# Causal mask of layer 1's key-major attention tiles: a GpSimd select on the exponentials in place of mask matmuls

## Chip, cores and metric

One core of one Trainium2 chip. The metric is the device time of one launch in microseconds (us), median of several runs.

## What is computed

Two layers, each `x + s * g`, on `x` of 2 x 1024 tokens and 128 channels. `s` is a 16-head attention with 8 channels a head over the layer-normed tokens, `g` the SiLU of a mixture of experts. The change touches `s` of layer 1 alone:

```
attn = jnp.einsum('bhqd,bhkd->bhqk', Q, K) * scale
causal = jnp.tril(jnp.ones((Sx, Sx), dtype=bool))
attn = jnp.where(causal, attn, jnp.asarray(-jnp.inf, dtype=attn.dtype))
probs = jax.nn.softmax(attn, axis=-1)
y = jnp.einsum('bhqk,bhkd->bhqd', probs, V)
return y @ W_O.T
```

## The kernel before

Every engine runs a program of its own, in the order in which it is written, and semaphores join them. `attention(l)` stands once for each engine. It works through 16 halves H (`HALVES`): a half is 512 queries of one group of four heads (`HG`), so that halves 2G and 2G+1 are the two query ranges of group G.

**Key-major steps.** `t_steps(1, H)` lists a half's steps. An even half has four, one for each tile of 128 keys from 0 to 3, and its rows narrow from 512 queries to 384, 256 and 128, since the queries that come before a key tile are left out. An odd half has eight: tiles 0 to 3 at the full 512 queries, then tiles 4 to 7 at 512, 384, 256 and 128. In the eight steps of a pair that start on the diagonal (all four of an even half, steps 4 to 7 of an odd one) the first 128 columns of each tile need the causal mask. In a step, for each head j:

- TensorE's `st_step` multiplies keys by queries into one of three PSUM banks (4 + m % 3). It waits until the exponential three tiles earlier has left that bank. In layer 1 a diagonal tile gets two more matmuls, `mask(...)`, of 64 rows and 128 columns each, which add -1e30 above the diagonal. Heads 0, 2 and 1, 3 lie in different halves of the array's rows.
- ScalarE (L776) takes the exponential of the tile from PSUM into `Pr`, eight slots of the arena, and counts `e_done`.
- TensorE's `av_step` multiplies V, with a column of ones, by the four exponentials of a step, in four column groups, into bank 7. It is issued one step late: after `st_step(H, i, 2)` TensorE issues `av_step` of the step before.

**Row maxima.** Two halves ahead, the same scores are computed query-major, so that each row's maximum is known: `s_unit` writes one of a ring of four banks (0 to 3), VectorE (L1079) reduces it and frees the bank. These tiles are masked by two matmuls too, with mask and identity changed over. `s_plan` cuts the stream of these units into the steps of each half, `unit_plan[l][H][i]`; TensorE issues them among `st_step` and `av_step`. After a half's last unit stands `("K", H)`, where VectorE joins the two maxima and GpSimd splits them into three bf16 parts (`max_parts`, L662 to L665), and four units later `("M", H)`, where TensorE transposes them (it waits for `mp_ready`); from there they go by DMA into rows of the queries.

**GpSimd in attention.** In each half it first copies V for the next group (`stage`, L648, even halves), then does `max_parts` of two halves ahead, and then `normalise` of the half before (L671), which waits for the inverse sums by DMA (`rb_in`). At the end of a half ScalarE moves bank 7 out (`evac`, L765); the first `av_step` of the next half waits for it.

The diagonal mask's lines in TensorE's program before:

```
masked = l == 1 and kt * P == q0
...
if masked:
    order = (identb, identb_sw) if row == 0 else (identb_sw, identb)
    masks = (mask_kq, mask_kq_sw) if row == 0 else (mask_kq_sw, mask_kq)
    ins = mask(bank(b_, 0, P), row, order, masks)
```

Of the kernel before, what the change touches and what calls it, by code (L numbers as in the profile page):

```python
# [162 lines left out]
def block_net(nc, a, out):  # L163
    ctx = ExitStack()
    with ctx:
# [3 lines left out]
        def sem(name):  # L169
            return ctx.enter_context(nc.semaphore(name))  # L170
# [14 lines left out]
        def bank(n, lo=0, hi=512):  # L185
            return PS[:, n * 512 + lo:n * 512 + hi]
# [85 lines left out]
        def gate_bufs(n):  # L272
# [71 lines left out]
            "ring_full", "ring_free", "st_ps", "e_done", "av_done", "o_ev", "mx_ready", "mp_ready", "v_staged",  # L344
            "sum_in", "sum_inv", "sum_out", "rb_in", "r_done", "pj_ps", "pj_ev")}
            for l in range(2)]
        h_ld = [sem(f"h_ld{s}") for s in range(2)]

        rw_in = [sem(f"rw_in{e}") for e in range(EXP)]
# [22 lines left out]
        def last_s(l, H):  # L372

            return max(place[l][w] for w in s_units(l, H)) + 1

        def two_before(l, H):

# [229 lines left out]
        def _(pool):  # L607
# [31 lines left out]
            def attention(l):  # L639
# [27 lines left out]
                def normalise(H):  # L667
# [2 lines left out]
                    pool.wait_ge(A["rb_in"], 16 * (H + 1))  # L670
                    g.tensor_tensor(OT[:, G, 512 * h:512 * (h + 1)], Osb[:, h, :], RB[l][:, h, :], ALU.mult).then_inc(A["r_done"], 1)  # L671

                stage(0)
                for H in range(LAG[l]):
                    max_parts(H)
                for H in range(HALVES):
                    if H % 2 == 0 and H // 2 + 1 < GROUPS:
                        stage(H // 2 + 1)
                    if H + LAG[l] < HALVES:
                        max_parts(H + LAG[l])  # L680
                    if H >= 1:
                        normalise(H - 1)
                normalise(HALVES - 1)

# [609 lines left out]
        def _(pe):  # L1294
# [57 lines left out]
            def attention(l):  # L1352
# [53 lines left out]
                def st_step(H, i, j):  # L1406
                    kt, off = t_steps(l, H)[i]
                    G, h, pr, row = H // 2, H % 2, j // 2, 64 * (j % 2)
                    m = HG * (steps_before(l, H) + i) + j

                    if m >= 3:
                        pe.wait_ge(A["e_done"], m - 2)
                    w = 512 - off
                    q0 = 512 * h + off
                    b_ = 4 + m % 3
                    extra = []
                    if l == 0 and h == 0 and kt == KT - 2:
                        extra = [(0, Hst[:, G % 2, j, part, 0:P]) for part in range(PARTS)]
                    if l == 0 and h == 0 and kt == KT - 1:
                        extra = [(q * P, Hst[:, G % 2, j, part, P * (1 - q):P * (2 - q)]) for q in range(2) for part in range(PARTS)]  # L1420
                    masked = l == 1 and kt * P == q0
                    ins = mm(bank(b_, 0, w), Ks[G][row:row + TROWS, pr, kt * P:(kt + 1) * P],
                             Qs[G][row:row + TROWS, pr, q0:q0 + w], stop=not (extra or masked))
                    for n, (c0, lhsT) in enumerate(extra):
                        ins = mm(bank(b_, c0, c0 + P), lhsT, flip[:, :], start=False, stop=n == len(extra) - 1)
                    if masked:
                        order = (identb, identb_sw) if row == 0 else (identb_sw, identb)
                        masks = (mask_kq, mask_kq_sw) if row == 0 else (mask_kq_sw, mask_kq)
                        ins = mask(bank(b_, 0, P), row, order, masks)
                    ins.then_inc(A["st_ps"], 1)  # L1430

                def av_step(H, i):
# [2 lines left out]
                    G = H // 2  # L1435
                    n = steps_before(l, H) + i
                    pe.wait_ge(A["e_done"], HG * (n + 1))
                    if i == 0:
                        pe.wait_ge(A["v_staged"], G + 1)
                        if H:  # L1440
                            pe.wait_ge(A["o_ev"], H)
# [225 lines left out]
```

## Time and profile before

| | us |
|---|---|
| median of 3 runs | 1474.37 (1468.91 to 1479.78) |
| the profiled execution's own time | 1461.52 |
| its span | 1459.7 |
| TensorE busy in it, matmuls | 1159.7 |
| VectorE busy | 921.6 |
| ScalarE busy | 695.6 |
| GpSimd busy | 198.7 |

Layer 1's attention runs from 894 to 1133 us of the span. In the rows below PE is TensorE, DVE VectorE, ACT ScalarE and POOL GpSimd; all of TensorE's tiled matmuls have the helper's line L1296, so they are told apart by their shapes: 51 rows are an `st_step` tile, 48 rows an `s_unit` tile, 64 rows a mask, 128 rows by 32 columns an `av_step`. A timeline row with a count covers what its engine issued from there on in that form, and its time then spans all of it. A matmul's time includes its way through the array, so that two that start 0.06 us apart each read 0.21 us. An idle time in brackets is that ahead of the instruction, with what ended it.

### The profile page before, as it was taken

How to read it: one execution, taken by the hardware profiler on the slowest of the kernel's cores; microseconds unless marked ns; L12 is line 12 of the kernel's file. 1: busy time of each engine (PE TensorE's matmuls, PEld its weight loads, DVE VectorE, ACT ScalarE, POOL GpSimd, SP SyncE). 2: the span in 40 equal slices, each digit the busy share in tenths (PEclk: the TensorE clock that was granted, in tenths of full speed). 3: DMA queues.
4: the chain of work that ended last, by engine and by line, in shares of the span. 5: the costliest groups of instructions: out<-in, count | busy, mean ns of one | idle time of the engine just before them, and what ended most of it. 6: DMA issues, size and time to landing. Idle time of an engine off the chain costs nothing.

```text
span 1459.7 us, 19168 instructions
## 1 busy us (share of the span) xinstructions
PE 1159.7 (79%) x6931; PEld 549.4 (38%) x6931; DVE 921.6 (63%) x1669; ACT 695.6 (48%) x1326; POOL 198.7 (14%) x292
## 2 busy tenths in 40 slices
PE   5699998578887888888787354999998597897477
PEld 3466665122221222222214222444442274464255
DVE  6678777557776776677606563878883055544577
ACT  5344445056665665566643303777776122121356
POOL 2155552000010001000100000111111300000200
PEclk9799999578998999899958556999998798898778
DMA  5512241401101101010003551000000600000050
GB/s 161 174 40 80 79 105 42 112 4 31 30 17 30 31 10 37 10 30 9 16 8 104 149 155 39 18 26 18 25 18 27 237 1 0 0 0 0 0 232 29
DMA packets 60995, 77.90 MB, mean 53 GB/s; under 512 B 15616, under 2 KB 39792, under 8 KB 57840
## 3 DMA queue, kind: packets, MB, share of 16 engines
q1 hardware_dynamic: 60912, 76.81, 16.9%
q8 instruction: 50, 0.82, 0.2%
q14 instruction: 33, 0.27, 0.1%
HBM read 61.58 MB, written 14.56 MB: 52 GB/s over the span
## 4 chain that ended last, share of the span: by engine, by line
PE 56%; DVE 16%; SPq 9%; issue 7%; ACT 6%; DMA 5%; DVEq 0%; POOL 0%; ACTq 0%; POOLq 0%
PE PS L1296 54%; DVE mx L1079 4%; SPq L457 3%; SPq L475 3%; ACT arena L776 3%; DMA arena<-mrow 3%; DVE g_hi_lo L1169 3%; SPq L464 1%; ACT g_hi_lo L827 1%; DVE w_hi_lo L1272 1%; SPq L442 1%; DVE arena L1281 1%; PE PS L1309 1%; DMA k_dram<-arena 1%; DVE fw L1182 1%
## 5 line engine op out<-in xcount | busy, mean ns | idle before, releaser
L1296 PE MATMUL PS<-arena 128*32 128x512 f32 (+12 forms) x3680 | 656.1, 508 | 146.8 <-DMA arena<-mrow 111.2
L1079 DVE TENSOR_REDUCE mx<-PS 128x1 f32<-128x512 f32 (+3 forms) x896 | 505.8, 624 | 217.4 <-PE PS L1296 213.4
L776 ACT ACTIVATE arena<-PS 128x512 f32<-128x512 f32 (+3 forms) x896 | 439.3, 557 | 357.3 <-PE PS L1296 354.9
L1296 PEld LDWEIGHTS PS<-arena 128*32 128x32 f32 (+3 forms) x3680 | 167.1, 107 | 531.9 <-DVE mx L1079 141.7
L1169 DVE TENSOR_TENSOR g_hi_lo<-fw,g_hi_lo 128x512 fp32r<-128x512 f32 x80 | 91.9, 1148 | 48.4 <-ACT g_hi_lo L827 48.2
L1296 PE MATMUL PS<-x_hi,w_hi_lo 128*128 128x512 f32 x320 | 113.6, 397 | 1.3 <-DVE fw L1182 0.9
L705 POOL TENSOR_TENSOR fw<-fw,arena 128x512 f32<-128x512 f32 x64 | 90.7, 1422 | 101.1 <-DVE fw L1182 101.1
L835 ACT ACTIVATE fw<-PS 128x512 f32<-128x512 f32 x80 | 47.8, 598 | 97.9 <-PE PS L1296 97.8
L1296 PE MATMUL PS<-g_hi_lo,w_hi_lo 128*128 128x512 f32 x240 | 75.5, 424 | 15.8 <-DVE g_hi_lo L1169 15.8
L1296 PE MATMUL PS<-e_hi_lo,w_hi_lo 128*128 128x512 f32 x192 | 61.8, 404 | 11.7 <-DVE e_hi_lo L1225 11.7
L662 POOL CAST mparts<-mneg 128x16 bf16<-128x16 f32 x24 | 4.7, 196 | 470.1 <-DVE mneg L1072 470.1
L1296 PEld LDWEIGHTS PS<-x_hi,w_hi_lo 128*128 128x128 f32 x320 | 60.9, 190 | 17.7 <-issue 1.3
L1296 PE MATMUL PS<-x_lo,w_hi_lo 128*128 128x512 f32 x160 | 63.5, 397 | 0.0
L1296 PEld LDWEIGHTS PS<-g_hi_lo,w_hi_lo 128*128 128x128 f32 x240 | 39.7, 188 | 47.0 <-DVE g_hi_lo L1169 42.3
L1182 DVE TENSOR_TENSOR fw<-PS,fw 128x512 f32<-128x512 f32 x80 | 54.3, 680 | 4.5 <-ACT fw L835 4.5
L1296 PE MATMUL PS<-identb_sw,mask_kq_sw 64*128 64x128 bf16 x256 | 55.6, 233 | 0.0
L1296 PE MATMUL PS<-identb,mask_kq 64*128 64x128 bf16 x256 | 54.2, 233 | 0.0
L1296 PE MATMUL PS<-e_hi_lo,fw_lo 128*128 128x512 f32 (+1 forms) x128 | 52.2, 408 | 0.0
L1296 PE MATMUL PS<-mask_kq,identb 64*128 64x128 bf16 x256 | 51.1, 220 | 0.0
L1296 PE MATMUL PS<-mask_kq_sw,identb_sw 64*128 64x128 bf16 x256 | 51.1, 220 | 0.0
L1309 PE MATMUL PS<-ident,arena 128*128 128x128 f32 x96 | 22.1, 401 | 35.6 <-DVE arena L967 27.9
L827 ACT ACTIVATE g_hi_lo<-fw 128x512 fp32r<-128x512 f32 x80 | 49.8, 623 | 0.8 <-DVE fw L1182 0.8
(219 smaller groups left out, 1171.6 us busy)
## 6 DMA issues: line engine op xcount, KB each, us to landing
arena<-comb_dram SPq DMA_DIRECT2D x24, 1024.0 KB, 7.8
arena<-k_dram SPq DMA_DIRECT2D x16, 408.0 KB
q_dram<-arena SPq DMA_DIRECT2D x24, 256.0 KB, 3.8
k_dram<-arena SPq DMA_DIRECT2D x24, 256.0 KB, 3.8
arena<-q_dram SPq DMA_DIRECT2D x16, 384.0 KB
arena<-drev_dram SPq DMA_DIRECT2D x32, 192.0 KB, 3.6
fw<-sum_dram SPq DMA_DIRECT2D x16, 256.0 KB
arena<-sum_dram SPq DMA_DIRECT2D x16, 256.0 KB
```

The source lines that it names most:

```text
L442: sp.dma_start(dst, src).then_inc(qk_stored[l][b], 16)
L457: sp.dma_start(dst, src).then_inc(att[l][f"ld{n}"], 16)
L475: sp.dma_start(dst, mrow[first:first + 12, H % 2, :]).then_inc(A["m_ld"], 16)
L705: g.tensor_tensor(g_, g_, cwb[:, slot, 512 * (u // 2):512 * (u // 2 + 1)], ALU.mult).then_inc(gw_made, 1)
L776: s.activation(Pr[:, m % 8, 0:w], bank(4 + m % 3, 0, w), ACT.Exp).then_inc(A["e_done"], 1)
L827: s.activation(g_r[0][:, u % 4, :], fg[:, u % 4, :], ACT.Copy).then_inc(ghi_made, 1)
L835: s.activation(fa[:, u % 2, :], bank(2 * (u % 2)), ACT.Silu).then_inc(a_made, 1)
L1079: v.reduce_max(mx[:, H % 2, kh, n:n + 1], bank(U % RING, 0, w), axis=AX.X, negate=True).then_inc(A["ring_free"], 1)
L1169: v.tensor_tensor(g_r[1][:, u % 4, :], fg[:, u % 4, :], g_r[0][:, u % 4, :], ALU.subtract).then_inc(glo_made, 1)
L1182: v.tensor_tensor(fg[:, u % 4, :], bank(2 * (u % 2) + 1), fa[:, u % 2, :], ALU.mult).then_inc(g_made, 1)
L1296: return nc.tensor.matmul(out_, lhsT, rhs, start=start, stop=stop)
L1309: ins = nc.tensor.transpose(bank(first + c, P * k, P * (k + 1)), src(4 * c + k), ident[:, :])
```

## The change

In layer 1 `st_step` issues no mask matmuls: the exponentials above the diagonal come out unmasked. After the four exponentials of a diagonal step, GpSimd runs one `affine_select` over the first 128 columns of the step's four slots of `Pr` (128 partitions, 4 x 128 numbers, f32, in place), which writes 0 where the key comes later than the query. It waits for `e_done` of all four heads and counts `causal_done`; `av_step` of a diagonal step waits for that count too. The query-major tiles keep their mask matmuls. GpSimd's program is rewritten so that the selects stand in step order: `max_parts` moves to the place of its `("K", H)` in the step plan, and layer 1's `normalise(H - 2)` of odd halves moves behind step 2 of half H.

```diff
+        causal_done = sem("causal_done")
...
+        def diagonal(H, i):
+
+            return H % 2 == 0 or i >= 4
+
+        def diagonals_before(H, i):
+            return sum(1 for K in range(H) for k in range(len(t_steps(1, K))) if diagonal(K, k)) + sum(
+                1 for k in range(i) if diagonal(H, k))
...
+                def causal(H, i):
+
+                    n = steps_before(1, H) + i
+                    pool.wait_ge(A["e_done"], HG * (n + 1))
+                    first = HG * n % 8
+                    block = Pr[:, first:first + HG, 0:P]
+                    g.affine_select(out=block, in_=block, compare_op=ALU.is_ge, fill=0.0, base=0,
+                                    pattern=[[0, HG], [1, P]], channel_multiplier=-1).then_inc(causal_done, 1)
+
                 stage(0)
-                for H in range(LAG[l]):
-                    max_parts(H)
+                for what in first_units[l]:
+                    if what[0] == "K":
+                        max_parts(what[1])
                 for H in range(HALVES):
                     if H % 2 == 0 and H // 2 + 1 < GROUPS:
                         stage(H // 2 + 1)
-                    if H + LAG[l] < HALVES:
-                        max_parts(H + LAG[l])
-                    if H >= 1:
+                    for i in range(len(t_steps(l, H))):
+                        if l == 1 and diagonal(H, i):
+                            causal(H, i)
+                        for what in unit_plan[l][H][i]:
+                            if what[0] == "K":
+                                max_parts(what[1])
+                        if l == 1 and H % 2 == 1 and i == 2 and H >= 2:
+                            normalise(H - 2)
+                    if H >= 1 and (l == 0 or H % 2 == 1):
                         normalise(H - 1)
                 normalise(HALVES - 1)
...
-                    masked = l == 1 and kt * P == q0
                     ins = mm(bank(b_, 0, w), Ks[G][row:row + TROWS, pr, kt * P:(kt + 1) * P],
-                             Qs[G][row:row + TROWS, pr, q0:q0 + w], stop=not (extra or masked))
+                             Qs[G][row:row + TROWS, pr, q0:q0 + w], stop=not extra)
...
-                    if masked:
-                        order = (identb, identb_sw) if row == 0 else (identb_sw, identb)
-                        masks = (mask_kq, mask_kq_sw) if row == 0 else (mask_kq_sw, mask_kq)
-                        ins = mask(bank(b_, 0, P), row, order, masks)
                     ins.then_inc(A["st_ps"], 1)
...
                     pe.wait_ge(A["e_done"], HG * (n + 1))
+                    if l == 1 and diagonal(H, i):
+                        pe.wait_ge(causal_done, diagonals_before(H, i) + 1)
```

TensorE's order in step 2 of half 0, before. Here `arena 128x256` and `128x128` that wait for `e_done1` are `st_step` tiles, those that wait for `ring_free1` are `s_unit` tiles, and `32x384` is `av_step` of step 1:

```order
L1296 MATMUL PS<-arena 128x256 [waits e_done1]
L1296 MATMUL PS<-mask_kq,identb 128x128
L1296 MATMUL PS<-mask_kq_sw,identb_sw 128x128
L1296 MATMUL PS<-arena 32x384 [waits e_done1]
L1296 MATMUL PS<-arena 32x384 x3
L1296 MATMUL PS<-arena 128x256 [waits e_done1]
L1296 MATMUL PS<-mask_kq_sw,identb_sw 128x128
L1296 MATMUL PS<-mask_kq,identb 128x128
L1296 MATMUL PS<-arena 128x512 [waits ring_free1]
```

The same place in TensorE's order now (the helper's line is L1321):

```order
L1321 MATMUL PS<-arena 128x256 [waits e_done1]
L1321 MATMUL PS<-arena 32x384 [waits causal_done,e_done1]
L1321 MATMUL PS<-arena 32x384 x3
L1321 MATMUL PS<-arena 128x256 [waits e_done1]
L1321 MATMUL PS<-arena 128x512 [waits ring_free1]
```

The two mask matmuls behind each `st_step` tile are gone, and the first `av_step` matmul has a second semaphore to wait for. Nothing else on TensorE has changed places.

GpSimd's order in halves 1 and 2, before: `stage`'s copy, `max_parts`, one `normalise` a half:

```order
L662 CAST mparts<-mneg 128x4x4 [waits mx_ready1]
L663 TENSOR_TENSOR mrest<-mneg,mparts 128x16 [waits pool_own]
L664 CAST mparts<-mrest 128x4x4 [waits pool_own]
L665 TENSOR_TENSOR mparts<-mrest,mparts 128x4x4 [waits pool_own]
L671 TENSOR_TENSOR arena<-arena 128x512 [waits rb_in1]
L648 COPY arena<-arena 128x32x8 [waits av_done1]
```

The same stretch now, from the selects of half 1's steps 4 and 5 to those of half 2's steps 0 and 1:

```order
L688 AFFINE_SELECT arena<-arena 128x4x128 [waits e_done1] x4
L671 CAST mparts<-mneg 128x4x4 [waits mx_ready1]
L672 TENSOR_TENSOR mrest<-mneg,mparts 128x16 [waits pool_own]
L673 CAST mparts<-mrest 128x4x4 [waits pool_own]
L674 TENSOR_TENSOR mparts<-mrest,mparts 128x4x4 [waits pool_own]
L688 AFFINE_SELECT arena<-arena 128x4x128 [waits e_done1] x2
L680 TENSOR_TENSOR arena<-arena 128x512 [waits rb_in1]
L657 COPY arena<-arena 128x32x8 [waits av_done1]
L688 AFFINE_SELECT arena<-arena 128x4x128 [waits e_done1] x2
```

The x4 are half 0's last two selects and half 1's first two. `max_parts` now stands between two selects of the same half, and `normalise` and `stage` between the last select of an odd half and the first of the next. At the end of half 13 the order is another one; all four of its selects stand ahead of the last `max_parts`:

```order
L688 AFFINE_SELECT arena<-arena 128x4x128 [waits e_done1] x4
L671 CAST mparts<-mneg 128x4x4 [waits mx_ready1]
L672 TENSOR_TENSOR mrest<-mneg,mparts 128x16 [waits pool_own]
L673 CAST mparts<-mrest 128x4x4 [waits pool_own]
L674 TENSOR_TENSOR mparts<-mrest,mparts 128x4x4 [waits pool_own]
L680 TENSOR_TENSOR arena<-arena 128x512 [waits rb_in1]
```

## Rows read from the trace of the kernel before

**Rows 1.** The chain of waits, odd halves, into step 5: start, us, what.

```profile
947.66 0.61 ACT arena L776
948.26 0.05 issue
948.31 2.11 PE PS L1296 x20
...
950.44 0.50 ACT arena L776
...
977.57 2.11 PE PS L1296 x20
```

**Rows 2.** Busy time by stretch: PE, PEld, DVE, ACT, POOL; granted clock; DMA.

```profile
894.00:1133.00 239.00, 227.84 (x2446) 104.78 (x2447) 174.50 (x396) 170.31 (x401) 32.74 (x77) 0.96 0.07 23
...
1000.00:1020.00 20.00, 19.25 (x234) 9.65 (x230) 16.16 (x36) 14.19 (x34) 4.54 (x11) 1.00 0.08 24
...
1100.00:1112.00 12.00, 10.09 (x100) 4.14 (x101) 8.12 (x27) 8.96 (x23) 1.54 (x3) 1.00 0.02 4
1112.00:1126.00 14.00, 13.43 (x59) 2.63 (x59) 1.46 (x5) 8.09 (x17) 2.54 (x2) 0.51 0.12 40
...
400.00:420.00 20.00, 15.44 (x97) 3.77 (x94) 12.96 (x25) 11.62 (x23) 2.49 (x6) 0.83 0.05 16
420.00:440.00 20.00, 17.61 (x128) 5.47 (x128) 15.43 (x28) 12.83 (x24) 2.10 (x5) 1.00 0.05 15
```

**Rows 3.** Timeline of TensorE, halves of 937 to 967 us: start, us.

```profile
948.31 0.33 PE L1296 MATMUL PS<-arena 51*128 51x384 bf16 x1
948.48 0.22 PE L1296 MATMUL PS<-mask_kq,identb 64*128 64x128 bf16 x1
948.54 0.21 PE L1296 MATMUL PS<-mask_kq_sw,identb_sw 64*128 64x128 bf16 x1
948.68 1.33 PE L1296 MATMUL PS<-arena 128*32 128x512 f32 x9
...
955.86 0.58 PE L1296 MATMUL PS<-arena 128*32 128x128 f32 x9
...
957.98 0.33 PE L1296 MATMUL PS<-arena 51*128 51x384 bf16 x1
...
958.56 1.39 PE L1296 MATMUL PS<-arena 128*32 128x512 f32 x10
...
962.57 0.23 PE L1296 MATMUL PS<-arena 51*128 51x128 bf16 x1
...
962.84 0.64 PE L1296 MATMUL PS<-arena 128*32 128x256 f32 x8
```

**Rows 4.** Timeline of ScalarE: the last exponential of an odd half.

```profile
954.34 0.28 ACT L776 ACTIVATE arena<-PS 128x128 f32<-128x128 f32 x1 [0.56 <-PE PS L1296]
```

**Rows 5.** GpSimd's groups by line: busy us, mean ns, idle before.

```profile
L671 POOL TENSOR_TENSOR arena<-arena 128x512 f32<-128x512 f32 x16 | 20.3, 1268 | 152.4 <-DMA arena<-sum_dram 152.4
...
L662 POOL CAST mparts<-mneg 128x16 bf16<-128x16 f32 x24 | 4.7, 196 | 470.1 <-DVE mneg L1072 470.1
...
L716 POOL CAST w_hi_lo<-fw 128x1024 fp32r<-128x1024 f32 x3 | 3.1, 1036 | 0.0
...
L627 POOL TENSOR_SCALAR_AFFINE_SELECT ident<-ident 128x128 f32<-128x128 f32 x1 | 0.3, 292 | 0.2 <-POOL ones L618 0.2
```

**Rows 6.** Timeline, end of half 13, all engines.

```profile
1099.30 0.20 POOL L662 CAST mparts<-mneg 128x16 bf16<-128x16 f32 x1 [9.82 <-DVE mneg L1072]
...
1099.66 0.28 ACT L776 ACTIVATE arena<-PS 128x128 f32<-128x128 f32 x1 [0.56 <-PE PS L1296]
...
1100.41 0.24 PE L1296 MATMUL PS<-identb,mparts 128*48 128x128 bf16 x1 [0.79 <-POOL mparts L665]
```

**Rows 7.** Timeline of TensorE in half 15, steps 2 and 3, at the lower clock.

```profile
1114.78 3.43 PE L1296 MATMUL PS<-arena 51*128 51x512 bf16 x12 [0.26 <-ACT arena L776]
1118.47 3.43 PE L1296 MATMUL PS<-arena 51*128 51x512 bf16 x12 [0.26 <-ACT arena L776]
```

## Prediction

> **What bounds the kernel now.** I read the chain of waits first, since TensorE is busy for 95% of layer 1's attention (227.8 of 239 us, [rows 2]) and a change that takes 512 matmuls from it looks like a gain. The chain shows what kind of busy that is [rows 1]: an exponential ends at 948.26, 0.05 us later TensorE starts the next `st_step` tile, 2.11 us of TensorE follow, then the next exponential, and so round. This is a loop of TensorE and ScalarE, once per step: the last exponential of a step (head 3) frees a bank, `st_step` of head 2 of the next step goes into it, `av_step` and the step's ring units follow, then `st_step` of head 3, whose exponential closes the loop. What stands between an exponential's end and `av_step` counts in full; masks of heads 0 and 1, which run beside head 3's exponential, count nothing. The same piece comes back at 977.57, 29.26 us later [rows 1]: a pair of halves, twelve steps, eight of them diagonal.
>
> The timeline gives the piece that the change rebuilds. Head 2's tile starts at 948.31, its masks at 948.48 and 948.54, `av_step` at 948.68: 0.37 us from tile to `av_step` where the tile is 384 wide, and 0.27 where it is 128 wide (962.57 to 962.84); a 256-wide one lies between, 0.32 [rows 3]. So before, `av_step` starts 0.42 us (0.05 + 0.37) after the exponential it waits for, or less.
>
> **What it removes.** 256 tiles lose a pair of masks. Two masks of one tile start 0.06 us apart [rows 3], so a pair holds its tile back by 0.12 us. On the loop stands head 3's pair, 8 x 0.12 = 0.96 us per pair of halves. One more counts: `av_step` of an odd half's step 3 isn't masked, but stands behind head 2's masked tile of step 4: 0.12. Head 2's other pairs stand ahead of an `av_step` that will wait for GpSimd anyway. Saved: 1.08 us per pair of halves. The plain count, 256 x 0.12 = 31 us, is what it would be if TensorE's issue alone were the bound.
>
> **What it adds.** In 64 steps `av_step` waits for exponential, then select, then `av_step`. The trace has no select of 4 x 128 numbers, so it is bounded: below by the 128-wide select, 0.29 us; above by GpSimd's two-input operation on as many numbers (512), 1.27 us [rows 5]. The value I take goes by the shape of the one-input operations: a CAST of 16 numbers a partition takes 196 ns and one of 1024 takes 1036, so 0.83 ns a number over 183 ns; that line gives 290 ns at 128, where the f32 select has 292. At 512 it gives 183 + 427 = 0.61 us.
>
> The Trainium skill (GPSIMD Engine Reference, section 3.1) speaks against this: it gives a GpSimd software loop at best about 1.8 cycles an element, with 769 ns measured for 512 elements. The trace's 1036 ns for 1024 numbers is 0.83 ns a number, where that rule would want 1.5, so I keep 0.61; by the rule each wait below grows by 0.16 us and the result by some 9 us.
>
> Hops: GpSimd starts 0.07 us after the instruction that it waits for and TensorE 0.05 us; both are my estimates from the 0.05 us in the chain [rows 1]. `av_step` can then start 0.07 + 0.61 + 0.05 = 0.73 us after the exponential's end, which is 0.68 after head 2's tile. Per pair of halves:
> - odd half, step 4: 0.68 - 0.37 = 0.31; step 5: 0.68 - 0.32 = 0.36; step 6: 0.68 - 0.27 = 0.41;
> - step 7: nothing. Its last exponential ends at 954.62 [rows 4], its `av_step` stands behind the wide tiles of the next half and comes at 955.86 [rows 3], long after 954.62 + 0.73;
> - even half, step 0: its `av_step` already waits for bank 7 to be emptied, 0.58 us after the tile (957.98 to 958.56, [rows 3]): 0.10; steps 1 to 3: 0.36, 0.41 and, by the mean of those, 0.35 with most of it passed on to VectorE, whose queue is just fed at that point: 0.32.
>
> Sum 2.27 us later, 1.08 earlier: +1.2 us a pair, +9.5 us for eight pairs. Behind the waiting `av_step` on TensorE stand the ring units and head 3's tile; ScalarE has heads 0 to 2 to do meanwhile and then runs dry as before, and VectorE empties its ring and runs dry earlier. That is why I see nothing that takes the delay up.
>
> **What it moves.** `max_parts` now stands behind the second select of a half. It takes 1.1 us (1099.30 to TensorE's start at 1100.41, [rows 6]) and is needed only in the step after, so it and the third select both fit: cost nothing, with about 0.2 us to spare. `normalise` (1.27 us, [rows 5]) waited for its DMA before and still does; it and `stage` fit between the last select of an odd half and the next. The one place that loses is the end of half 13: there `max_parts` is on TensorE's path already (0.79 us of wait, [rows 6]) and now stands behind the select of step 7. The exponential ends at 1099.94; 0.07 + 0.61 for the select and 1.1 for `max_parts` bring the transposition to 1101.75 in place of 1100.41: +1.3 us. On SP nothing moves; its waits shift with the rest, and the weights' loads behind attention shift too.
>
> **The clock.** In this stretch TensorE is granted all of its clock with 19.25 of 20 us busy; in 1112 to 1126 it is at 0.51, the lower level of 1.2 GHz, after a stretch busy for 10.1 of 12 us [rows 2]. At the lower level a 512-wide step takes 3.69 us (1114.78 to 1118.47, [rows 7]) against about 2.6. Halves 14 and 15 now have waits in each diagonal step and fewer matmuls, so I expect the fall a few us earlier and the return later: some three narrow steps and two wide ones at 0.7 to 1.1 us each, about +4 us, with 0 to 8 as bounds.
>
> **Sum.** 9.5 + 1.3 + 4 = +14.8 us on the profiled execution: 1461.5 to 1476.3. The median shown is 13 us above that execution, which stands near the lowest run; I carry the same difference over: 1474.4 + 14.8 = 1489 us.
>
> **Rivals.**
> - *A longer select.* A pattern of four pieces with gaps may cost more than the plain rows. At 0.85 us, a third of the way from my value to the upper bound, the seven waits of a pair grow by 0.24 us each: +13 us more, 1502 us. At the upper bound of 1.27 us it would be +37, 1526. The fit of 292 ns on the line of the casts speaks against it; that no row has a select in pieces speaks for it.
> - *The clock falls in the main stretch too.* In layer 0's attention stretches with 15.4 of 20 us busy have 0.83 of the clock, one with 17.6 has 1.00 [rows 2]. Here seven waits of some 0.3 us a pair and fewer matmuls leave about 17 of 20 us busy (28.2 less 2.1 us in 30.4), between the two. If each pair had one fall as in layer 0, some 7 us at 3.69 in place of 2.6 us a step, that would be 2 us a pair: +16 and more, 1505 to 1510 us. The Trainium skill (TensorE: Matmul & The Clock Gate, Part 1) says that "the default state is throttled, and activity releases the throttle"; by it masks, too, were activity, which is on this rival's side.
> - *The select costs little, and the sign turns.* The mechanism is the same wait, priced at the 0.29 us of the 128-wide select. Then `av_step` may start 0.36 us after head 2's tile, and the seven waits sum to 0.3 us against 1.08 saved: -6.2 us for eight pairs, +1 at half 13, without the clock's part 1469 us. The point from which it decides is a select of 0.44 us: seven waits 0.17 us shorter than mine. Slack that I haven't seen (ring units that TensorE could do sooner) would lead to the same place, 1465 to 1480.
> - *TensorE's issue is the bound.* Then the 31 us of masks go, with the waits of 18 us (8 x 2.27) hidden or not: 1443 to 1461 us. The busy share speaks for it, the chain, which names ScalarE in every diagonal step, against it.
>
> **Chances.** A measurement here can tell about 1%, 15 us, from no change. Forecast (1482 to 1497 us) 0.42, about half of it on either side of +1%; longer select 0.17; clock in the main stretch 0.18; cheap select or slack 0.15, within 1% but for 0.02; issue-bound 0.08, of it 0.06 faster. Slower by over 1%: 0.21 of the forecast, 0.17 and 0.17 of the next two, 0.55. Faster by over 1%: 0.02 + 0.06 = 0.08. Within 1%: the rest, 0.37. The forecast's own range is 1482 to 1497; the range that should hold 8 in 10 goes from 1469, the cheap select, to 1512, the clock in the main stretch with a rest of the longer select.
>
> **What would show it.** Right: a select of 0.6 us on GpSimd, `av_step` of diagonal steps 0.7 us after its last exponential, a pair of halves of 30.4 us, and TensorE's `mparts` transposition at the end of half 13 waiting 2 us. Wrong: a select below 0.45 us, `av_step` of diagonal steps no later than now, or a pair of halves at or below 29.26 us; a granted clock below 1.00 between 905 and 1100 us would make it the clock rival.

## The result and the profile after

Before 1471.64 us (1464.34 to 1479.78, four runs), after 1506.45 us (1497.24 to 1522.45, four runs): ratio 1.021, 95% interval 1.013 to 1.030. The change makes the kernel slower by some 35 us, where +15 was forecast. The profiled execution after took 1497.24 us (span 1495.5), 35.7 more than the one before. The ratios and intervals, here and below, leave out runs in the chip's slower state (here the one of 1522.45), so they differ a little from the quotients of the medians.

The page of after: busy time by engine, and the row of the new select (mean 635 ns; before it GpSimd idles for ScalarE's exponentials).

```profile
PE 1175.9 (79%) x6419; PEld 533.9 (36%) x6419; DVE 923.3 (62%) x1669; ACT 695.0 (46%) x1326; POOL 238.4 (16%) x356
...
L688 POOL TENSOR_SCALAR_AFFINE_SELECT arena<-arena 128x512 f32<-128x512 f32 x64 | 40.6, 635 | 192.9 <-ACT arena L801 192.9
```

TensorE issues 512 matmuls fewer and is still busy for 16 us more (1159.7 before): part of what it has left runs at a lower clock. First the wait that was added. The chain of waits after, over the end of an odd half and the next even one; it answers to [rows 1]:

```profile
957.10 0.39 ACT arena L801
957.50 0.06 issue
957.56 0.65 POOL arena L688
958.21 0.14 issue
958.34 4.86 PE PS L1321 x40
963.20 0.02 issue
963.23 0.60 ACT arena L801
963.83 0.07 issue
963.89 0.65 POOL arena L688
964.54 0.09 issue
964.63 2.52 PE PS L1321 x10
```

GpSimd stands in the loop now: exponential, 0.06, select 0.65, 0.14, TensorE. Step 4 of an odd half in after's timeline answers to [rows 3]:

```profile
951.97 0.33 PE L1321 MATMUL PS<-arena 51*128 51x384 bf16 x1 [0.28 <-ACT arena L801]
951.99 0.63 POOL L688 TENSOR_SCALAR_AFFINE_SELECT arena<-arena 128x512 f32<-128x512 f32 x1 [5.02 <-ACT arena L801]
...
952.74 0.19 PEld L1321 LDWEIGHTS PS<-arena 128*32 128x32 f32 x8 [0.68 <-ACT arena L801]
...
952.77 0.64 PE L1321 MATMUL PS<-arena 128*32 128x512 f32 x4 [0.46 <-ACT arena L801]
```

From head 2's tile to `av_step` it is 0.80 us (951.97 to 952.77), against 0.37 in [rows 3]. The brackets name ScalarE, whose exponential had ended before 951.97: the releaser is the select, which ends last, at 952.62.

Windows after, which answer to [rows 2]: layer 1's attention, then the stretch in which before ran at full clock, then pieces.

```profile
893.00:1173.00 280.00, 240.12 (x1933) 87.57 (x1933) 176.28 (x396) 169.50 (x400) 72.01 (x141) 0.79 0.07 23
905.00:1100.00 195.00, 169.48 (x1503) 68.10 (x1500) 140.59 (x309) 123.11 (x288) 53.21 (x106) 0.86 0.06 18
934.00:957.00 23.00, 19.55 (x184) 7.39 (x184) 18.35 (x40) 15.37 (x36) 5.94 (x14) 1.00 0.07 18
957.00:975.00 18.00, 16.08 (x124) 6.97 (x123) 9.64 (x24) 9.20 (x25) 6.22 (x12) 0.53 0.04 12
...
1128.00:1172.00 44.00, 35.52 (x160) 6.57 (x158) 11.03 (x35) 22.56 (x56) 9.27 (x16) 0.51 0.13 46
```

The same stretch in before:

```profile
905.00:1100.00 195.00, 187.51 (x2121) 89.26 (x2120) 158.05 (x348) 142.83 (x334) 27.83 (x69) 1.00 0.07 21
```

TensorE is busy for 169.5 of 195 us where it was for 187.5, and its granted clock is 0.86, not 1.00. It falls to the lower level, 1.2 GHz, again and again: TensorE was busy for 19.6 of 23 us at full clock before the fall at 958, and 16.1 of 18 us at the low one, in which VectorE is busy for 0.54 of the time and ScalarE for 0.51, where they had been for 0.80 and 0.67.

At the end of half 13, which answers to [rows 6], `max_parts` stands behind the select of step 7, and TensorE's transposition waits 2.08 us for it in place of 0.79. GpSimd's timeline after:

```profile
1130.88 0.64 POOL L688 TENSOR_SCALAR_AFFINE_SELECT arena<-arena 128x512 f32<-128x512 f32 x1 [1.83 <-ACT arena L801]
1131.46 0.20 POOL L671 CAST mparts<-mneg 128x16 bf16<-128x16 f32 x1
...
1132.31 0.22 POOL L674 TENSOR_TENSOR mparts<-mrest,mparts 128x16 bf16<-128x16 f32 x1
```

and TensorE's, with two wide steps of half 15 at the low clock, 3.74 us apart ([rows 7] had 3.69):

```profile
1132.58 0.30 PE L1321 MATMUL PS<-identb,mparts 128*48 128x128 bf16 x1 [2.08 <-POOL mparts L674]
...
1147.59 3.48 PE L1321 MATMUL PS<-arena 51*128 51x512 bf16 x12 [0.26 <-ACT arena L801]
1151.33 3.43 PE L1321 MATMUL PS<-arena 51*128 51x512 bf16 x12 [0.26 <-ACT arena L801]
```

### The profile page after: what moved, and what is told of

It is laid out like the page before. It is cut to its first block, busy times and chain, and to the rows that moved or that the text cites. A ratio compares the mean times of both kernels' runs of the same rounds, so it can differ in the third digit from the quotient of the medians.

```text
span 1495.5 us, 18272 instructions
## 1 busy us (share of the span) xinstructions
PE 1175.9 (79%) x6419; PEld 533.9 (36%) x6419; DVE 923.3 (62%) x1669; ACT 695.0 (46%) x1326; POOL 238.4 (16%) x356
## 4 chain that ended last, share of the span: by engine, by line
PE 54%; DVE 17%; SPq 9%; ACT 8%; issue 6%; DMA 4%; POOL 2%; DVEq 0%; ACTq 0%; POOLq 0%
PE PS L1321 52%; DVE mx L1104 5%; ACT arena L801 5%; SPq L466 3%; DMA arena<-mrow 3%; SPq L484 3%; DVE g_hi_lo L1194 2%; POOL arena L688 1%; ACT g_hi_lo L852 1%; SPq L473 1%; DVE w_hi_lo L1297 1%; SPq L451 1%; PE PS L1334 1%; DMA k_dram<-arena 1%; DVE arena L1306 1%
## 5 line engine op out<-in xcount | busy, mean ns | idle before, releaser
L1321 PE MATMUL PS<-arena 128*32 128x512 f32 (+12 forms) x3680 | 679.3, 536 | 171.1 <-DMA arena<-mrow 109.5
L1321 PEld LDWEIGHTS PS<-arena 128*32 128x32 f32 (+3 forms) x3680 | 170.0, 111 | 591.2 <-ACT arena L801 165.1
L1194 DVE TENSOR_TENSOR g_hi_lo<-fw,g_hi_lo 128x512 fp32r<-128x512 f32 x80 | 91.9, 1148 | 47.8 <-ACT g_hi_lo L852 47.6
L1321 PE MATMUL PS<-x_hi,w_hi_lo 128*128 128x512 f32 x320 | 114.0, 398 | 0.8 <-DVE combT L1053 0.4
L860 ACT ACTIVATE fw<-PS 128x512 f32<-128x512 f32 x80 | 47.8, 598 | 97.8 <-PE PS L1321 97.8
L1321 PE MATMUL PS<-g_hi_lo,w_hi_lo 128*128 128x512 f32 x240 | 75.5, 423 | 15.9 <-DVE g_hi_lo L1194 15.9
L1321 PE MATMUL PS<-e_hi_lo,w_hi_lo 128*128 128x512 f32 x192 | 62.5, 408 | 12.0 <-DVE e_hi_lo L1250 12.0
L688 POOL TENSOR_SCALAR_AFFINE_SELECT arena<-arena 128x512 f32<-128x512 f32 x64 | 40.6, 635 | 192.9 <-ACT arena L801 192.9
L1321 PEld LDWEIGHTS PS<-x_hi,w_hi_lo 128*128 128x128 f32 x320 | 61.1, 191 | 17.5 <-issue 1.1
L1321 PE MATMUL PS<-x_lo,w_hi_lo 128*128 128x512 f32 x160 | 63.6, 398 | 0.0
L1321 PE MATMUL PS<-identb_sw,mask_kq_sw 64*128 64x128 bf16 x256 | 57.7, 253 | 0.0
L1321 PEld LDWEIGHTS PS<-g_hi_lo,w_hi_lo 128*128 128x128 f32 x240 | 39.7, 188 | 47.1 <-DVE g_hi_lo L1194 42.5
L1321 PE MATMUL PS<-identb,mask_kq 64*128 64x128 bf16 x256 | 56.4, 253 | 0.0
L1321 PE MATMUL PS<-e_hi_lo,fw_lo 128*128 128x512 f32 (+1 forms) x128 | 52.5, 410 | 0.0
L1334 PE MATMUL PS<-ident,arena 128*128 128x128 f32 x96 | 21.7, 397 | 35.9 <-DVE arena L992 28.2
L913 ACT ACTIVATE e_hi_lo<-arena 128x1024 fp32r<-128x1024 f32 x16 | 17.0, 1060 | 65.9 <-PE PS L1321 43.6
```

The costliest lines, as they stand in the source:

```text
L688: g.affine_select(out=block, in_=block, compare_op=ALU.is_ge, fill=0.0, base=0, pattern=[[0, HG], [1, P]], channel_multiplier=-1).then_inc ...
L860: s.activation(fa[:, u % 2, :], bank(2 * (u % 2)), ACT.Silu).then_inc(a_made, 1)
L1194: v.tensor_tensor(g_r[1][:, u % 4, :], fg[:, u % 4, :], g_r[0][:, u % 4, :], ALU.subtract).then_inc(glo_made, 1)
L1321: return nc.tensor.matmul(out_, lhsT, rhs, start=start, stop=stop)
L1334: ins = nc.tensor.transpose(bank(first + c, P * k, P * (k + 1)), src(4 * c + k), ident[:, :])
```

## Experiments

How the runs are read. The first `av_step` of layer 1 comes between 895.7 and 913.9 us in these kernels' traces, for reasons that lie ahead of what was changed, so single spans say little. Three numbers are taken from each trace: the **stage**, from the first to the last `av_step` of layer 1; the **pair**, twelve steps at full clock, as the sum of the median distance between successive `av_step` at each of the twelve places; and **low**, the time of the stage at 1.2 GHz. The medians are of device times, each against before's runs of the same chip: 1471.64 for after, 1466.69 for e1 to e4, 1466.91 for e5 to e8, 1468.78 for e9 to e12.

| kernel | pair | stage | low | median, us | ratio (95%) |
|---|---|---|---|---|---|
| before | 29.26 | 232.8 | 15.1 | | |
| after | 31.54 | 274.5 | 110.7 | 1506.45 | 1.021 (1.013 to 1.030) |
| e1_no_mask | 27.97 | 228.3 | 37.2 | 1457.76 | 0.994 (0.990 to 0.998) |
| e2_both | 32.29 | 265.9 | 44.1 | 1490.91 | 1.014 (1.010 to 1.018) |
| e3_masks01 | 31.54 | 263.8 | 62.3 | 1496.54 | 1.016 (1.009 to 1.022) |
| e4_split | 29.30 | 241.6 | 47.1 | 1483.01 | 1.010 (1.006 to 1.014) |
| e5_late_av | 28.71 | 249.0 | 75.0 | 1483.17 | 1.010 (1.006 to 1.014) |
| e6_before_late_av | 30.06 | 241.8 | 28.0 | 1482.40 | 1.011 (1.003 to 1.018) |
| e7_split_late | 28.71 | 247.3 | 73.3 | 1482.04 | 1.013 (1.006 to 1.019) |
| e8_double | | 337.7 | 218.2 | 1564.19 | 1.068 (1.062 to 1.075) |
| e9_hybrid_split | 28.52 | 246.4 | 72.4 | 1480.23 | 1.008 (1.004 to 1.013) |
| e10_hybrid_split_masks01 | 28.62 | 233.4 | 35.5 | 1466.18 | 0.997 (0.992 to 1.001) |
| e11_before_hybrid | 29.54 | 240.9 | 36.1 | 1468.21 | 1.000 (0.996 to 1.004) |
| e12_one_wait | 30.96 | 263.0 | 78.7 | 1488.74 (one run) | |

After's own trace has too little full clock for two of the twelve places; the other ten agree with e3's, so its pair is e3's.

**e1: neither masks nor selects.** The kernel leaves the causal mask of the key-major tiles out; GpSimd's new order stays.

```diff
-                        if l == 1 and diagonal(H, i):
-                            causal(H, i)
...
-                    if l == 1 and diagonal(H, i):
-                        pe.wait_ge(causal_done, diagonals_before(H, i) + 1)
```

> Neither mask matmuls nor selects: the causal mask of the key-major tiles is left out of the computation, GpSimd's new order stays. Loop theory: only the masks of head 3 and of step 4's head 2 stood on the loop, so a pair of halves shortens by 8 x 0.12 + 0.12 = 1.1 us, 29.3 to 28.2, and the run by 8.6 us against before (ratio 0.994). TensorE's issue as the bound: 256 x 0.12 = 31 us less (0.979). Clock theory: masks are activity too; without them the granted clock falls in the main stretch at some ends of an odd half although nothing waits for GpSimd, and the gain is eaten up: ratio 0.994 to 1.005, mean clock of the attention stretch below before's 0.96.

The pair is 27.97 us: the masks were worth 29.26 - 27.97 = 1.29 us a pair, and the waits of the change cost 31.54 - 27.97 = 3.57. What is gained is small, 9 us of 1467 with 512 matmuls gone and nothing in their place. The stage gives only 4.5 us for a loop that is 8 x 1.29 = 10 us shorter, since 22 us more of it run at 1.2 GHz. All of its time at 1.2 GHz but the first 1.7 us lies behind 1090.6, in halves 13 to 15. The fall in the main stretch that the clock theory expected of e1 didn't come:

```profile
905.00:1100.00 195.00, 178.79 (x1726) 70.33 (x1723) 164.14 (x370) 145.64 (x347) 29.37 (x71) 0.98 0.07 21
```

So taking the masks away doesn't by itself lose the clock there.

**e2 and e3: after's waits, with masks back.** e2 has all mask matmuls back beside the selects, e3 those of heads 0 and 1, which lie beside head 3's exponential.

```diff
+                    masked = l == 1 and kt * P == q0          # e3: ... and j < 2
...
-                             Qs[G][row:row + TROWS, pr, q0:q0 + w], stop=not extra)
+                             Qs[G][row:row + TROWS, pr, q0:q0 + w], stop=not (extra or masked))
...
+                    if masked:
+                        order = (identb, identb_sw) if row == 0 else (identb_sw, identb)
+                        masks = (mask_kq, mask_kq_sw) if row == 0 else (mask_kq_sw, mask_kq)
+                        ins = mask(bank(b_, 0, P), row, order, masks)
```

> The changed kernel with the mask matmuls put back: masks and selects both. The waits for GpSimd stay, TensorE has before's activity. Loop theory alone (clock of no importance): 1.1 us a pair slower than the changed kernel, +8.6 us. Clock theory: the clock stays at 1.00 from 905 to 1130 us; the waits cost 7 x 0.45 us a pair against before at full clock, +25 us on 1460 us of span, so some 1485 to 1490 us of span, 6 to 10 us less than the changed kernel's 1495.5 although it does more work.

> The changed kernel with the mask matmuls of heads 0 and 1 alone put back, which run beside head 3's exponential; the selects stay. Loop theory: these matmuls cost nothing and gain nothing, ratio to the changed kernel 1.00. Clock theory: they are half of the activity that was taken away, off the loop; the clock falls in fewer places, and the run is 5 to 15 us faster than the changed kernel at the same pair of halves of 31.5 us.

Both do more work than after and have a stage that is shorter, by 8.6 and 10.7 us. In e2 the pair is 0.75 us longer, which should have made the stage 6 us longer; the clock is back at its upper level at 915.1, just behind the first `av_step` at 913.7, and doesn't fall once before 1137. The windows of e2, then of e3:

```profile
905.00:1100.00 195.00, 170.12 (x1886) 81.46 (x1886) 142.48 (x314) 126.74 (x294) 52.22 (x106) 0.97 0.06 17
```

```profile
905.00:1100.00 195.00, 170.41 (x1692) 74.57 (x1688) 141.00 (x309) 124.62 (x294) 53.71 (x110) 0.91 0.06 18
```

With the waits in all three, e2, e3 and after issue 1886, 1692 and 1503 matmuls in the 195 us, for much the same busy time (170.1, 170.4 and 169.5 us), at a clock of 0.97, 0.91 and 0.86. What e2 lacks to 1.00, and more than half of what e3 lacks, is the time until the clock first rises (915.1 and 927.2). Behind it, up to the end of the sixth pair, e2 has no time at 1.2 GHz, e3 13.7 us and after 54.3 us. Once the waits are there, the masks hold the clock. With e1 the square is full: where only the masks are gone (e1) or only the waits are added (e2), the clock stays up in the main stretch; where both were done, as in after, it falls. The count alone is no rule across kernels: without masks in both, e12 issues 1561 in the same window at 0.92, e9 1636 at 0.91. The medians' intervals overlap after's, so by the times alone e2 and e3 would show nothing; the stages in the traces do, with one trace a kernel (e2's is of its slowest execution, 1506.11 us).

**e4: a cheaper wait.** The select is cut in two, heads 0 to 2 while head 3's exponential still runs, then head 3 alone.

```diff
-                    pool.wait_ge(A["e_done"], HG * (n + 1))
...
-                    g.affine_select(out=block, in_=block, compare_op=ALU.is_ge, fill=0.0, base=0,
-                                    pattern=[[0, HG], [1, P]], channel_multiplier=-1).then_inc(causal_done, 1)
+                    for lo, hi in ((0, 3), (3, 4)):
+                        pool.wait_ge(A["e_done"], HG * n + hi)
+                        block = Pr[:, first + lo:first + hi, 0:P]
+                        g.affine_select(out=block, in_=block, compare_op=ALU.is_ge, fill=0.0, base=0,
+                                        pattern=[[0, hi - lo], [1, P]], channel_multiplier=-1).then_inc(causal_done, 1)
...
-                        pe.wait_ge(causal_done, diagonals_before(H, i) + 1)
+                        pe.wait_ge(causal_done, 2 * diagonals_before(H, i) + 2)
```

> The changed kernel with each select in two: heads 0 to 2 (3 x 128 numbers) as soon as they are there, then head 3 alone (128 numbers, 0.29 us). Loop theory: av_step then comes 0.07 + 0.29 + 0.15 = 0.51 us after the last exponential in place of 0.85, seven waits of 0.34 us a pair: 2.4 us a pair, 19 us, plus what the clock gives back: span 1470 to 1478. If the select's length were not what counts (a queue on GpSimd, say), no change or slower, since GpSimd has 64 more instructions.

GpSimd's groups by form in e4, and the chain into step 5 of an odd half:

```profile
L689 POOL TENSOR_SCALAR_AFFINE_SELECT arena<-arena 128x384 f32<-128x384 f32 x64 | 33.4, 523 | 101.4 <-ACT arena L802 101.4
L689 POOL TENSOR_SCALAR_AFFINE_SELECT arena<-arena 128x128 f32<-128x128 f32 x64 | 18.8, 294 | 39.9 <-ACT arena L802 39.8
```

```profile
950.09 0.50 ACT arena L802
950.59 0.06 issue
950.65 0.30 POOL arena L689
950.95 0.14 issue
951.09 1.33 PE PS L1322 x10
```

Only the short select is behind the last exponential, and `av_step` starts 0.50 us after it (950.59 to 951.09) where after has 0.85. The pair falls by 2.24 us to 29.30, before's own. Yet the kernel stays 16 us slower than before. Its stage is 8.8 us longer with the same pair, and 32 us more of it run at 1.2 GHz, most of that in halves 14 and 15. The six executions part in two groups that go with the clock of the whole launch: 1467.6 (the one traced) and 1468.0 us at 0.849 and 0.852, the other four 1481.0 to 1486.6 us at 0.835 to 0.838. So the price of the waits alone is not the slowdown.

**e5, e6, e7: `av_step` one head later.** `av_step` goes behind head 3's `st_step` tile, where the select is long done; in after (e5), in before (e6), in e4 (e7).

```diff
-                            if j == 2 and before:
+                            if j == (3 if l == 1 else 2) and before:
```

> The changed kernel with av_step of layer 1 issued after st_step of head 3 in place of head 2 (one index in TensorE's order). Loop theory: the wait for GpSimd then no longer stands between an exponential and the next head-3 tile; head 3's tile needs only the exponential of head 0 of its own step, so the 2.3 us a pair of the waits and some of the av_step itself leave the loop, and a pair of halves takes what e1 has (28.0) or less: span 1440 to 1460, ratio to before 0.985 to 1.00, with the clock the better the fuller TensorE is. If GpSimd's select were a bound in itself, or the delayed av_step starved the ring units behind it as much as before, no change from the changed kernel (ratio 1.02).

> Control: the kernel before (masks on TensorE, no selects) with the same move of av_step. Loop theory: av_step leaves the loop here too; a pair of halves falls from 29.3 to what TensorE's order and VectorE's ring allow, 27 to 28.5; ratio 0.98 to 0.995. If it is as fast as e5, the select has no merit of its own; if it stays at 29.3, TensorE's issue was the bound and the masks cost what they take there.

> e4 and e5 together: select split 3 + 1, av_step after head 3's tile. Loop theory: the select's end is then always ahead of av_step; equal to or up to 0.5% faster than e5, and the fastest of the four: span 1440 to 1455. Clock theory: the shorter the waits, the fewer falls.

None of the three gains that were expected came. The move takes 2.83 us off after's pair (28.71), and then the split is worth nothing (28.71): the select is hidden. In before it costs 0.80 (30.06); the largest piece is at the `av_step` of step 7, 3.65 us from the one ahead of it against 2.47, of which the next place gives back 0.64. And e5 and e7, whose loop is 0.55 us a pair shorter than before's, take 15 to 16 us more than before. They spend 75 and 73 us at 1.2 GHz. For e5 and e7 the loop's cost at full clock is excluded as the cause, since it has the other sign.

**e9, e10, e11: the decisive pair.** The move is kept for diagonal steps except the one at the change of halves (e9, on e4's split); e10 is e9 with the masks of heads 0 and 1 back, as in e3; e11 is the move in before.

```diff
-                            if j == 2 and before:
+                            if before and j == (3 if l == 1 and diagonal(*before) and not (H % 2 == 0 and i == 0) else 2):
```

> The changed kernel, select split 3 + 1, av_step moved behind head 3's tile only for diagonal steps, and not in an even half's first step, where e5 to e7 lost 1.3 us a pair (3.54 to 3.65 us in place of 2.24 to 2.47). Loop theory: off the loop in the narrow steps, and the lost 1.3 us back: a pair of halves of 27.4 to 28.2 us at full clock, a gain of 9 to 15 us at full clock on before (ratio 0.990 to 0.995); each fall of the clock in the main stretch takes 2 to 3 us of it. If the move only shifts the wait elsewhere, 28.7 as in e7.

> e9 with the mask matmuls of heads 0 and 1 put back. Loop theory: the same or 0.3 us more a pair of halves than e9 at full clock. Clock theory: no fall in the main stretch; ratio to before 0.990 to 0.996 and at least as good as e9's, though TensorE does 256 matmuls more. If the clock's falls do not depend on the masks, e10 is 0 to 3 us slower than e9.

> Control: the kernel before, masks on TensorE, with e9's move of av_step alone. Loop theory: av_step leaves the loop of the narrow steps here too: 28.4 to 29.0 us a pair, ratio 0.992 to 1.000. If it equals e9 and e10, the select is worth nothing beyond the move; if the select is worth its masks, it is 1 us a pair slower than e9 at full clock.

e9 and e10 differ by 256 matmuls that compute nothing that is needed, and their pairs by 0.1 us. The windows of e9, then of e10:

```profile
905.00:1100.00 195.00, 176.67 (x1636) 69.28 (x1637) 152.90 (x337) 134.94 (x319) 63.30 (x162) 0.91 0.07 19
```

```profile
905.00:1100.00 195.00, 182.23 (x1959) 79.22 (x1955) 160.92 (x355) 142.43 (x342) 69.43 (x179) 1.00 0.07 20
```

e9's clock falls twice in the main stretch, for 17 us each (at 928 and 993), e10's doesn't fall before 1104.8, where half 14 is about to begin. e9 itself missed its forecast: its pair is 28.52 us for an expected 27.4 to 28.2, and its ratio 1.008 for 0.990 to 0.995. e10's stage is 13.0 us shorter and its median of ten runs 14.1 us lower; the intervals don't meet. Over these ten runs each, e9's mean clock of the whole launch is 0.838 and e10's 0.850, where before's is 0.851. One edit that only adds work, and costs 0.1 us a pair in the loop, takes 1% off the time. It also gives the best kernel with selects, at before's time and not measurably below it (0.992 to 1.001), though its pair is 0.6 us shorter than before's: the end of the stage, at 1.2 GHz for 35 us against 14, gives that back. e11 shows that the move by itself is no gain for before (ratio 1.000, a pair of 29.54 us where 28.4 to 29.0 was expected), so e10 isn't measurably better than e11 either.

**e8: the select twice.** A second select ahead of each, so that the wait grows by a known amount.

```diff
+                    own.link(g.affine_select(out=block, in_=block, compare_op=ALU.is_ge, fill=0.0, base=0,
+                                             pattern=[[0, HG], [1, P]], channel_multiplier=-1))
```

> The changed kernel with every select run twice, the second waiting for the first (its result is the same). Loop theory: each of the seven waits a pair that show grows by 0.63 + 0.07 = 0.7 us: a pair of halves from 31.5 to 36.4 at full clock, some 0.7 x 57 = 40 us, and the clock falls more: span 1535 to 1560. If the cost of the change came from the clock or from GpSimd's order and not from the select's length, under 10 us.

`av_step` comes 1.55 us after the exponential, 0.70 later than in after; where two steps in a row are at full clock (steps 4 of odd halves) their distance grows by that, 3.73 us against 3.02. Seven waits of 0.70 make a pair of 31.5 + 4.9 = 36.4 us. The measured pairs are 41 to 44 us:

```profile
905.00:1100.00 195.00, 156.26 (x1190) 61.60 (x1187) 115.31 (x248) 100.64 (x233) 63.23 (x116) 0.71 0.05 14
```

At a clock of 0.71, every us of added wait brings more than itself. By the medians, each against before on its own chip, e8 adds 97.3 us where after adds 34.8; that is 62.5 us more (the stage is 63.2 longer) for 8 x 4.9 = 39 us of wait.

**e12: one semaphore.** The select waits for the exponentials itself, so TensorE's first wait is not needed.

```diff
-                    pe.wait_ge(A["e_done"], HG * (n + 1))
                     if l == 1 and diagonal(H, i):
                         pe.wait_ge(causal_done, diagonals_before(H, i) + 1)
+                    else:
+                        pe.wait_ge(A["e_done"], HG * (n + 1))
```

> The changed kernel, where av_step of a diagonal step waits for causal_done alone (the select itself waited for the four exponentials, so e_done is implied). The changed kernel's trace has 0.145 us from the select's end to av_step, 0.09 more than TensorE takes from the end of a last exponential to its next tile. If the second semaphore of the pair costs it, 0.06 us in place of 0.145 and 0.6 us a pair less (31.5 to 30.9); if it belongs to the weight load that now stands behind the wait, or to GpSimd's semaphore, 0.145 as before.

The timeline of e12, step 5 of an odd half:

```profile
953.64 0.63 POOL L688 TENSOR_SCALAR_AFFINE_SELECT arena<-arena 128x512 f32<-128x512 f32 x1 [2.26 <-ACT arena L801]
...
954.33 0.16 PEld L1321 LDWEIGHTS PS<-arena 128*32 128x32 f32 x8 [0.61 <-POOL arena L688]
954.33 0.85 PE L1321 MATMUL PS<-arena 128*32 128x384 f32 x8 [0.42 <-POOL arena L688]
```

From the select's end (954.27) to `av_step` it is 0.054 us, where after has 0.145. The pair falls by 0.58 us, nearly 7 x 0.09 = 0.63. It isn't the number of semaphores that counts: at step 0 of an even half e12's `av_step` waits for three (the select's, V's copy and the emptied bank) and starts 0.054 us behind the select as well. By the trace's record of each instruction's semaphores, in the seven places of every pair, after waits for the select in an instruction of its own ahead of `av_step`'s weight load, and the load carries the wait for `e_done`; in e12 the weight load itself waits for the select. Its time is one run and isn't ranked against the others.

## Why the forecast was right in sign and short in size

The forecast said slower, +14.8 us, and 1506 lies within its range; the size was under half of the measured one. By the stage, after's excess over before is 274.5 - 232.8 = 41.7 us; in the profiled executions 5.8 of it came back outside the stage (1.4 ahead of it, 4.4 behind), which leaves the span's 35.8.

| term | forecast | measured |
|---|---|---|
| masks saved, a pair | 1.08, and 0.6 in the waits' baseline | 1.29 |
| waits added, a pair | 2.27 over before's `av_step`, 2.9 over e1's | 3.57 over e1's |
| eight pairs | +9.5 | 8 x 2.28 = +18.2 |
| half 13's transposition | +1.3 | 2.08 - 0.79 = +1.3 |
| clock, main stretch | 0 (a rival: 2 a pair, 16) | +13.3 |
| clock, end | +4 (0 to 8) | +8.9 |
| outside the stage | 0 | -5.8 |

The clock's main term is the first six pairs of after, 203.1 us, less 6 x 31.54, less the 0.6 by which before's first six exceed 6 x 29.26. The end's is what remains: 41.7 - 18.2 - 1.3 - 13.3.

**What bounds the kernel.** Right. The loop of TensorE and ScalarE sets the pair. e1 gives 10 us for eight pairs where issue as the bound would give 31.

**The sum of the loop was mis-sized**, by 1.09 us a pair (2.28 for 1.19), at two steps. The first is the wait. Its hop from select to TensorE was taken as 0.05 us and measured 0.145 (0.10 at step 0 of an even half); without the wait for `e_done` beside it, it is 0.054 (e12), so 0.09 is what the wait in an instruction of its own costs. The chain's 0.05 in [rows 1] belongs to a tile whose weight load does the waiting; mine had two waits, and the late one stood apart. With a select of 635 ns for 0.61, `av_step` comes 0.85 us after the exponential for the forecast's 0.73: 0.7 us over the seven places (3.57 for 2.9). The second is the masks. I had head 3's pairs in the 1.08 and head 2's in the baseline, since each wait was counted from before's 0.42 us and not from the 0.32, 0.27 and 0.21 us that e1 has without masks. Together that is 14 mask pairs at 0.12 us, 1.7 us a pair of halves, where all masks of it were worth 1.29: the remaining 0.4. A mask pair on the loop thus held it back by 0.09 us in the mean, less than the 0.12 that two starts make. Step 7's wait is nothing, as forecast. By place, the distance of `av_step` from the one before it, medians at full clock:

| kernel | even 0 | 1 | 2 | 3 | odd 4 | 5 | 6 | 7 |
|---|---|---|---|---|---|---|---|---|
| before | 2.69 | 2.36 | 1.92 | 1.80 | 2.61 | 2.63 | 2.08 | 2.47 |
| e1, nothing | 2.69 | 2.21 | 1.70 | 1.72 | 2.48 | 2.40 | 1.95 | 2.24 |
| e3, as after | 2.87 | 2.80 | 2.34 | 2.13 | 3.02 | 2.99 | 2.59 | 2.24 |

**The select's price** held within 4%: three sizes measured 294, 523 and 635 ns for 128, 384 and 512 numbers a partition, about 0.9 ns a number. The longer select as a rival falls. The 1.8 cycles an element that I had set against it from the Trainium skill (GPSIMD Engine Reference, section 3.1), with 769 ns for 512, don't hold for this operation, which took 635. The section gives them for loop bodies with k ≥ 3, in its words; for k ≤ 2 it has 1.03 cycles, by its 1.2 GHz an estimate of 0.86 ns an element, and with that the measured (635 - 294) / 384 = 0.89 ns a number agrees.

**What is moved** cost nothing, as forecast: the third select, behind `max_parts`, adds 2.59 - 1.95 = 0.64 us, which is 0.85 less e1's 0.21 and nothing more. Only the end of half 13 lost.

**The clock is the step that failed.** I took a busy share of about 17 of 20 us, put between two stretches of layer 0 with 15.4 (0.83) and 17.6 (1.00), and chose that the clock would stay; I gave its fall 0.18. It fell six times in the first six pairs, once after a stretch with 19.6 of 23 us busy, the same 17 of 20. The rival's price was good: 2 us a pair forecast, 13.3 / 6 = 2.2 measured. Its total of 1505 to 1510 holds the 1506 measured, but partly by luck: the waits were 8.7 us short in it too and the end 4.9, while 5.8 came back elsewhere and before's own median came out 2.7 lower than the one it starts from (1471.64 for 1474.37). At the end of the stage the clock stays low for 47.8 us, not the 13.7 of before, where I had counted five steps.

e9 against e10 shows that it is the clock and not something else that goes with it: the added matmuls cost 0.1 us a pair at full clock, and stage and median fall by 13 and 14 us with the clock's return. But the masks' going loses the clock in the main stretch only together with the rest of the change: e1 takes away the masks alone and e2 adds the waits alone, and neither loses it there. The sentence of the Trainium skill that I had set beside the rival (TensorE: Matmul & The Clock Gate, Part 1: activity releases the throttle) is borne out by e2 and e10: mask matmuls that do nothing for the result, and of which e10's stand beside other engines' work, keep the clock up between its first rise and half 14.

Four things stay open. What decides whether the clock falls in one kernel and not in another wasn't found: without masks in both, e12 has 0.92 of it with 1561 matmuls and 168.2 us busy in the 195, e9 0.91 with 1636 and 176.7. What halves 14 and 15 would need to keep the clock wasn't tried; all kernels lose it there. How much of the time goes when the clock is low was only worked out, not set: 13.3 us lost in 54 us at 1.2 GHz over after's first six pairs, a quarter. And why `av_step` of step 7 loses 1.2 to 1.3 us when it goes behind head 3's tile (e5, e6) wasn't taken apart; the hybrids only avoid it.

## What to carry to other kernels

Matmuls that lie beside another engine's work cost little, and together with short waits they may be what holds TensorE's clock; before taking them out and adding a wait, look at the granted clock of stretches with the busy share that will be left, and price the fall as a term of the sum, not as a rival. A wait that goes through one more engine costs the operation and two hops, and is to be counted from where the waiting instruction would stand without what is removed. Let the last engine wait for the new step's semaphore alone where that one implies the other, cut the step so that only a short piece follows the last input, and issue other work ahead of the instruction that waits.

## What the runs showed of the hardware

- `av_step` started 0.145 us after the select's end where TensorE waited for it in an instruction ahead of the weight load, and 0.054 us after it where the weight load itself did, at step 0 of an even half too, with two more semaphores to wait for (after, e12).
- GpSimd's affine select took 294, 523 and 635 ns for 1, 3 and 4 pieces of 128 f32 numbers a partition (e4, after), 0.9 ns a number; no run has 512 in one piece. Done twice, the second starts 0.07 us after the first (e8).
- TensorE at 1.2 GHz in a loop of several engines lost about a quarter of the time, not half: 13.3 us in 54, and a wide step took 3.74 us for some 2.65 (after). That the waits for the other engines don't stretch is my reading of it.
- The clock fell six times in after's first six pairs and came back each time, with 17 of 20 us busy in the loop and TensorE's matmuls never more than 0.57 us apart. 256 light matmuls more in 64 steps held it (e9: 0.91, e10: 1.00). In e1, with no waits for GpSimd and `av_step` in its old place, it held in the main stretch without any of them.
